# Eight fronts of a Mamba layer run first, with u, z and the dt, B, C rows kept in memory

## What is computed

```
xn    = rmsnorm(x)                       # 512 wide
u, z  = split(xn @ in_proj.T)            # 1024 wide each
u     = silu(causal_conv4(u))
dt_r, B, C = split(u @ x_proj.T)         # 32, 16, 16 wide
dt    = softplus(dt_r @ dt_proj.T + b)
h_t[n] = exp(dt*A[n]) * h_(t-1)[n] + dt*B_t[n]*u_t      # for 16 states n
y     = (sum_n h_t[n]*C_t[n] + u*D) * silu(z)
h     = x + y @ out_proj.T
h     = h + (silu(rmsnorm(h) @ w1.T) * (rmsnorm(h) @ w2.T)) @ w3.T
```

## Time and profile before

| | |
|---|---|
| median of 3 runs | 3673.43 us (3672.25 to 3678.02) |
| profiled execution | 3670.03 us, span 3668.2 us |
| PE, DVE, POOL, ACT busy | 3004.8, 2788.1, 2532.7, 2141.0 us |
| bytes moved | 497.9 MB, 136 GB/s over the span |

### The profile page before, as it was taken

How to read it: one execution, slowest core, us unless ns; L and a number is a source line. 1 busy time by engine, 2 the same in 40 slices (tenths; PEclk the granted TensorE clock), 3 DMA queues, 4 the chain that set the end, 5 groups by cost and what they waited for, 6 DMA issues and landing times. The chain is left out here.

```text
span 3668.2 us, 32780 instructions
## 1 busy us (share of the span) xinstructions
PE 3004.8 (82%) x8248; PEld 1452.7 (40%) x8248; DVE 2788.1 (76%) x3376; ACT 2141.0 (58%) x4823; POOL 2532.7 (69%) x1132
## 2 busy tenths in 40 slices
PE   6711389867986899899996899999998799999868
PEld 3200134333433444444443344444443344554444
DVE  3878889988888798879897788877898898322353
ACT  5544475567556775777558675667557756441332
POOL 0699969987988598876987677776798798300000
PEclk8855699978997999999997999999999799999979
DMA  4433445544554444554642444453555354212100
GB/s 158 122 115 127 147 142 192 171 137 153 177 169 124 133 150 141 174 166 133 203 167 93 154 135 141 157 172 135 159 175 170 123 175 143 101 42 88 39 1 23
DMA packets 225430, 497.91 MB, mean 136 GB/s; under 512 B 32348, under 2 KB 32732, under 8 KB 224988
## 3 DMA queue, kind: packets, MB, share of 16 engines
q1 hardware_dynamic: 225244, 495.82, 41.7%
HBM read 485.76 MB, written 9.96 MB: 135 GB/s over the span
## 5 line engine op out<-in xcount | busy, mean ns | idle before, releaser
L1080 POOL TENSOR_TENSOR hb<-hb,bc 128x1024 f32<-128x1024 f32 x512 | 1206.2, 2356 | 436.2 <-ACT state L1195 219.1
L1070 POOL TENSOR_TENSOR hb<-dtu,bc 128x1024 f32<-128x1024 f32 x512 | 1206.5, 2356 | 111.8 <-DVE ps L1435 107.0
L1127 ACT ACTIVATE ps<-dt,a_neg 128x512 f32<-128x512 f32 x1024 | 691.5, 690 | 687.2 <-DVE hb L1425 685.0
L1651 PE MATMUL ps<-fT,wden 128*128 128x512 f32 x2304 | 1036.2, 605 | 52.5 <-DVE dt L1413 7.5
L1425 DVE TENSOR_TENSOR_SCAN hb<-ps,hb 128x512 f32<-128x512 f32 x512 | 596.7, 1207 | 108.9 <-POOL hb L1070 96.6
L1651 PEld LDWEIGHTS ps<-fT,wden 128*128 128x128 f32 x2304 | 439.8, 194 | 600.1 <-issue 593.1
L1425 DVE TENSOR_TENSOR_SCAN hb<-ps,state,hb 128x512 f32<-128x512 f32 x512 | 627.2, 1266 | 65.5 <-POOL hb L1070 41.7
L1435 DVE TENSOR_TENSOR ps<-ps,hb 128x1024 f32<-128x1024 f32 x512 | 624.3, 1219 | 12.2 <-POOL hb L1080 11.8
L1651 PE MATMUL ps<-xnT,wmix 128*128 128x512 f32 x1024 | 456.7, 601 | 126.0 <-DMA wmix<-in_w_mix 113.4
L1741 PE MATMUL ps<-wden,hm 128*128 128x512 f32 x1024 | 456.2, 597 | 28.8 <-DVE res L1481 12.4
L1702 PE MATMUL ps<-wmix,u 128*128 128x512 f32 x512 | 241.2, 626 | 147.5 <-issue 82.0
(11 more groups left out here) (242 smaller groups left out, 3504.5 us busy)
## 6 DMA issues: line engine op xcount, KB each, us to landing
bc<-bc_dram SPq DMA_DIRECT2D x1024, 256.0 KB, 3.3
wden<-in_w SPq DMA_DIRECT2D x192, 512.0 KB, 3.9
wmix<-in_w_mix SPq DMA_DIRECT2D x128, 512.0 KB, 3.9
watt<-in_w_qof SPq DMA_DIRECT2D x26, 512.0 KB, 4.1
stage<-in_x SPq DMA_DIRECT2D x8, 1024.0 KB, 5.8
res<-in_x SPq DMA_DIRECT2D x8, 1024.0 KB, 6.6
wden<-in_w_qof SPq DMA_DIRECT2D x16, 512.0 KB, 4.2
out<-res SPq DMA_DIRECT2D x8, 1024.0 KB, 5.0
```

Of the source, the lines that this page charges most:

```text
L1070: TTn(hb[:, n % HB], dtu[:, :, :], bc[:, 0, n % BC].unsqueeze(1).broadcast_to([P, 2, CH]), ALU.mult).then_inc(s.s1_ready, 1)
L1080: TTn(hb[:, n % HB], hb[:, n % HB], bc[:, 1, n % BC].unsqueeze(1).broadcast_to([P, 2, CH]), ALU.mult).then_inc(s.s3_done, 1)
L1127: A_(dst, dt[:, p % 2, jj], ACT.Exp, scale=a_neg[:, j, n:n + 1]).then_inc(full_of(key), 1)
L1651: ins = M(dst, a, b, start=start and n == 0, stop=stop and n == len(pairs) - 1)
```

## The change

The z half of the input projection becomes a part of the front: after "proj" each front makes 8 z products, with tanh and product ("zg") as parts of the stream "f". All eight fronts come before the first output stage in that stream, with the key and value products after the first. What they make has to wait longer, so it goes to DRAM:

- a ring of two 512-wide slots (`ring`) takes the tanh of each "cvu" and "zg", the gated z, and for chunks from 2 on the dt, B, C rows. `ring_store` writes gated z to `z_dram` and the rows to `p_dram`; the next user but one of a slot waits, on ACT, until that store has landed (`ring_empty`);
- from chunk 2 on, u goes into the residual buffers `res[:, 1:3]` (`u_out`), from there to `u_dram` (`u_store`, pair by pair), and is read back into `u` (`u_load`) when the output projection has read that half of `u` for chunk c - 2;
- `z_load` reads the gated z of a pair into its place in `u` when the skip product of the pair and dt*u have been made, for the gate;
- `p_load` reads the dt rows back for chunks from 2 on; `load_b` and `load_c` read from `p_dram`;
- the third weight slot, for z, is gone: z weights go through the two slots of the fronts (`FSLOTS`);
- the residual x of chunks 1 and 2 is loaded after the last front, and "out" of chunk 0 waits for the last z product, as it shares `stage` and `xnT` with the fronts;
- the dt product waits for the skip product of the pair before, or for ACT's part of the block before.

`WORK`, `PHASE` and `LOOK` have new values, so the order of all streams is planned anew. The diff, cut to its core:

```diff
+RING = 2
@@ front
-    return got + [("proj", c)]
+    got.append(("proj", c))
+    for j in range(JB + 1):
+        got += [("z", c, j)] if j < JB else []
+        got += [("zg", c, j - 1)] if j else []
+    return got
@@ f_plan
-    got = front(0) + front(1)
+    got = []
+    for c in range(CHUNKS):
+        got += front(c)
+        if c == 0:
+            got += [("key", 0, c4) for c4 in range(KC)] + [("value", 0, b) for b in range(BATCH)]
     for c in range(CHUNKS):
...
         got += [("rms", c), ("hs", c)] + [("to", c, n) for n in range(KC)]
-        got += front(c + 2) if c + 2 < CHUNKS else []
@@ l_plan
-        for j in (2 * p, 2 * p + 1):
-            got += [("z", c, j), ("zt", c, j), ("zg", c, j)]
@@ planner's constants
-WORK = {"x": 1534.0, "w": 127.4, "s": 422.9, "y": 661.5, "f": 650.3}
+WORK = {"x": 849.2, "w": 145.7, "s": 1219.5, "y": 59.6, "f": 162.7}
-LOOK = {"m": 0.379, "l": 0.018, "x": 0.019, "w": 0.041, "s": 0.247, "y": 0.171, "f": 0.0}
+LOOK = {"m": 0.319, "l": 0.0, "x": 0.0, "w": 0.043, "s": 0.009, "y": 0.096, "f": 0.0}
@@ loads
+    for u, n in RING_AT.items():
+        if u[0] != "cvu":
+            at(DONE[u], 1, "ring_store", u)
+    for c in range(CHUNKS):
+        for p in range(PAIRS):
+            at(max(DONE[("yp", c, p)], DONE[("zg", c, 2 * p + 1)] + 4), 1, "z_load", c, p)
+            if c > 1:
+                at(DONE[("cvu", c, 2 * p + 1)], 2, "u_store", c, p)
+                at(max(DONE[("ou", c - 2, 1, p)], DONE[("cvu", c, 2 * p + 1)] + 4), 2, "u_load", c, p)
+        if c > 1:
+            at(max(DONE[("dt", c - 2, JB - 1)], DONE[("proj", c)] + 4), 2, "p_load", c)
@@ SBUF and DRAM
-        wmix = sb("wmix", [P, FSLOTS + 1, 1024])
+        wmix = sb("wmix", [P, FSLOTS, 1024])
+        ring = sb("ring", [P, RING, CH])
+        u_out = res[:, 1:3].rearrange("p r t d -> p (r t) d")
-        bc_dram = nc.dram_tensor("bc_dram", (2, 2 * NS, CH), f32, kind="Internal").ap()
+        p_dram = nc.dram_tensor("p_dram", (CHUNKS, 96, CH), f32, kind="Internal").ap()
+        u_dram = nc.dram_tensor("u_dram", (CHUNKS, PAIRS, P, 2, CH), f32, kind="Internal").ap()
+        z_dram = nc.dram_tensor("z_dram", (CHUNKS, PAIRS, P, 2, CH), f32, kind="Internal").ap()
@@ SP
+            def store_ring(unit):
...
+                sp.dma_start(dst, src).then_inc(ring_out[RING_AT[unit] % RING], 16)
@@ ACT
                 elif kind == "cvu":
                     act.wait_ge(s.conv_done, c * JB + i + 1)
-                    if i >= 2:
-                        emptied(act, ("u", c, i - 2))
-                    A_(th[:, i % 2], ps[:, USE[("u", c, i)][0]], ACT.Tanh).then_inc(s.th_ready, 1)
+                    ring_empty(act, unit)
+                    A_(ring_slot(unit), ps[:, USE[("u", c, i)][0]], ACT.Tanh).then_inc(s.th_ready, 1)
...
-                elif kind == "zt":
+                elif kind == "zg":
                     src = filled(act, ("z", c, i))
...
+                    ring_empty(act, unit)
+                    A_(ring_slot(unit), src, ACT.Tanh, scale=0.5).then_inc(s.zt_ready, 1)
                 elif kind == "out":
                     emptied(act, ("out", c, i))
                     if i == 0:
-                        filled(act, ("z", c, JB - 1))
+                        filled(act, ("z", CHUNKS - 1, JB - 1))
@@ DVE
                 elif kind == "gate":
                     summed(dve, c * STEPS + NS * i + NS - 1)
+                    dve.wait_ge(zg_in[i], 16 * (c + 1))
...
-                    V.scalar_tensor_tensor(u[:, half, i], zt, 1.0, ps[:, USE[key][0]], ALU.add, ALU.mult
+                    V.scalar_tensor_tensor(ring_slot(unit), ring_slot(unit), 1.0, ps[:, USE[key][0]], ALU.add, ALU.mult
@@ PE, dt
+                    if i % 2:
+                        pe.wait_ge(s.w_ready, c * JB + i)
+                    elif c or i:
+                        n, p = pair_of(c * PAIRS + i // 2 - 1)
+                        filled(pe, ("yp", n, p, 1))
```

More of the change, by code:

```diff
@@ L81, in l_plan, with ring_plan, ring_free @@
     got = sp_plan(0, 0) + sp_plan(0, 1)
-    for n in range(CHUNKS * PAIRS):
+    for n in range(1, CHUNKS * PAIRS):
         c, p = pair_of(n)
-        for j in (2 * p, 2 * p + 1):
-            got += [("z", c, j), ("zt", c, j), ("zg", c, j)]
-        if n + 1 < CHUNKS * PAIRS:
-            c, p = pair_of(n + 1)
-            got += sp_plan(c, 2 * p) + sp_plan(c, 2 * p + 1)
-    return got
+        got += sp_plan(c, 2 * p) + sp_plan(c, 2 * p + 1)
+    return got
+def ring_plan():
+    uses = []
+    for u in f_plan():
+        if u[0] in ("cvu", "zg") or u[0] == "proj" and u[1] > 1:
+            uses.append(u)
+    return {u: n for n, u in enumerate(uses)}, uses
+RING_AT, RING_USE = ring_plan()
+def ring_free(u):
+    n = RING_AT[u] - RING
+    if n < 0:
+        return None
+    old = RING_USE[n]
+    return old if old[0] == "cvu" else ("ring_out", old)
 def swiglu(c):
@@ L102, in y_plan @@
 def y_plan():
-    got = [("key", 0, c4) for c4 in range(KC)] + [("value", 0, b) for b in range(BATCH)]
+    got = []
     for c in range(CHUNKS):
@@ L217, in parts @@
     elif kind == "gate":
-        part(DVE, 1.5, ("zg", c, 2 * i + 1), ("sum", c, NS * i + NS - 1))
+        part(DVE, 1.5, ("z_load", c, i), ("z_kept", c, i), ("sum", c, NS * i + NS - 1))
     elif kind == "ou":
@@ L858, in f_in, with ring_slot, ring_stored, ring_empty @@
             return wmix[:, n % FSLOTS]
-        def z_in(eng, n):
-            eng.wait_ge(wz_in, 16 * (n + 1))
-            return wmix[:, FSLOTS]
+        def ring_slot(unit):
+            return ring[:, RING_AT[unit] % RING]
+        def ring_stored(eng, unit):
+            n = RING_AT[unit]
+            stored = [m for m in range(n % RING, n + 1, RING) if RING_USE[m][0] != "cvu"]
+            eng.wait_ge(ring_out[n % RING], 16 * len(stored))
+        def ring_empty(eng, unit):
+            n = RING_AT[unit] - RING
+            if n < 0:
+                return
+            old = RING_USE[n]
+            if old[0] == "cvu":
+                emptied(eng, ("u", old[1], old[2]))
+            else:
+                ring_stored(eng, old)
+        def u_there(eng, c, p):
+            if c > 1:
+                eng.wait_ge(u_in[p], 16 * (c - 1))
+            else:
+                for j in (2 * p, 2 * p + 1):
+                    emptied(eng, ("u", c, j))
+        def proj_kept(eng, c):
+            if c > 1:
+                ring_stored(eng, ("proj", c))
+            else:
+                eng.wait_ge(s.proj_stored, 16 * (c + 1))
         def y_in(eng, n):
@@ L1683, in _ @@
                         emptied(pe, ("u", c, j))
-                        ins = M(dst, wx[:, j], u[:, half, j], start=j == 0, stop=j == JB - 1)
+                        ins = M(dst, wx[:, j], u_out[:, j] if c > 1 else u[:, half, j], start=j == 0, stop=j == JB - 1)
                     ins.then_inc(full_of(key), 1)
```

177 lines of the change are left out of this document (113 added, 64 removed), and 10 rows, old and new, of the table PHASE.

## The result

The changed kernel takes 3610.1 us (median of 4 runs, 3603.7 to 3617.4), beside 3672.8 for the kernel before: a ratio of 0.983, with an interval of 0.980 to 0.985. The forecast was 3607 us. The sum is right within 3 us, and that closeness is partly luck: two of its terms were off by 27 and 18 us, in opposite directions, and the profiled execution, 3614.1 us, lies 10 above the 3604 that was forecast for it. The rest of this document is about these terms, and about a rival that was weighed by a rule that the runs overturn.

A forecast was written before the change was run, and what follows sets the result against it. No engine is full; scans, delayed 26 us by each front, then PE's tail set the end. 3670 - 21 (scans) - 45 (tail) = 3604, with the runs' median 3.4 above: 3607 us, range 3500 to 3745.

The forecast's parts named there:

- a rival that was weighed by a rule that the runs overturn: Fronts end late and delay chunk 2, from 6.2 us per z product on; near no change, 3668 us; chance 0.08.
- What chunks 0 and 1 cost: Scans of chunks 0 and 1, with seven fronts and z beside them: 822 us instead of 695, chunk 2 starting at 910.
- The prediction's lower bound: Chunks 0 and 1: fronts partly fit DVE's free 17%, each costing 14 us; scans end 100 us earlier than forecast.
- Chunks 2 to 6 then lose a front each: Later scans: 26 us less per chunk, 1995 to 1865 us; with chunk 7 and z given back, 2222 for chunks 2 to 7.
- Tail 45 us shorter: After the scans: 47 us of foreign PE work leaves chunk 7's dense stage; tail 45 us shorter, between 0 and 60.
- A front of 88 us: Fronts beside chunks 0 and 1: 61 us without z plus 27.6 for z; seven fronts end near 725 us.
- there is room until 910, 21 us a front: Between the fronts' end near 725 us, plus 35 for chunk 0's output stage, and chunk 2's start: 21 us spare a front.
- the prediction's own threshold of 109 us a front: Fronts of 88 us with 21 us of room each: late fronts cost time only from 6.2 us per z product on.
- New transfers: nothing, as long as they aren't late: DMA for z and u: 59 MB and 156 more issues on SP cost nothing if on time; uncovered u about 35 us once.
- The ring: Two-slot ring in the fronts: no bound; rival that ACT is held by its stores, 154 us, 3761 us; chance 0.31 with other order-made waits.
- The price of 3.0 us for a 256 KB store: Ring stores: 3.0 us on a line between 64 KB (2.5) and 1024 KB (5.0); slot turn somewhat over 4.4 us.
- The "much faster" rival: Scans and tail both gain: six chunks at 350 us end the scans 120 us earlier, 3487 us; chance 0.11.

The follow-up runs named there:

- The products left out: Changed kernel with the second of each four products of the last feed-forward matrix (128 dense products) left out: 3571.7 us, ratio 0.972 to the kernel before.
- run with z twice: Changed kernel with each z product of fronts 1 to 7 made twice by PE, order untouched: 3746.4 us, ratio 1.021 to the kernel before.
- run with the norm ahead: Changed kernel with norm and turning of the next front planned ahead of this front's z products: 3601.5 us, ratio 0.981 to the kernel before.
- the old values: Changed kernel with the WORK, PHASE and LOOK values of the kernel before, so another order of all queues: 3741.7 us, ratio 1.020.
- four slots: Changed kernel with a ring of four slots instead of two, planned order untouched: 3605.9 us, ratio 0.982 to the kernel before.
- one tap less: One of three DVE convolution taps left out, order untouched: changed kernel 3588.3 us (ratio 0.978), kernel before 3660.1 us (0.997).
- tiny transfers: Changed kernel with 80 extra 4 KB memory-to-memory transfers beside the u stores and the u and z loads: 3613.1 us, ratio 0.985.

## Why the prediction was right, and where its steps failed

The forecast of a small gain, with the tail as its main place, held. That the sum came within 3 us of the median is luck: the scans ended 27 us later than forecast against the kernel before, and the tail was 18 shorter. Its steps one by one:

1. **What chunks 0 and 1 cost: right in the sum, less so in its parts.** 822 against 821 us, from 26 us a front, 16 for z and 20 for other dense work. Two windows of the changed kernel, from the first dt*u to the last z tanh and from there to chunk 2, show where it was lost:

```profile
92.00:820.00 728.00, 555.86 (x1236) 245.91 (x1236) 612.10 (x675) 462.26 (x848) 523.42 (x226) 0.87 0.56 184
820.00:913.50 93.50, 74.55 (x177) 32.87 (x176) 79.78 (x79) 50.70 (x76) 92.12 (x42) 0.93 0.68 217
```

At 2.29 us for a POOL instruction, 226 of them leave 210 us of the first window, for 198 forecast for seven fronts and z. In the second POOL keeps the free pace although the dense stage of chunk 0 has begun: the 20 us put down for it weren't paid. To count a front's cost in windows in which one runs was the right way. The prediction's lower bound, 14 us from DVE's free share, would have been wrong by 100 us.

2. **"Chunks 2 to 6 then lose a front each", 130 us, and 18 for z: the mis-sized term.** They and chunk 7 lost 124 (2374 to 2250), not 148. By chunk it was 24, 6, 31, 35 and 25 us, each where 29 were forecast, and 2 in chunk 7 where 3 were forecast for its z. The one that falls out is chunk 3, which took 387 us after 393. What has changed beside it is the dense work: the feed-forward products of chunk 1 ran from 854 to 1124 us, in chunk 2, and now run from 1125 to 1361, so into chunk 3, and the means of the first batch entry begin at 1424 instead of 1175 us. So a row less its front isn't a row of the new kernel: dense work that has been put off comes in. But chunk 2 got such work too (758 PE instructions for 722, though its front is gone) and still gained 24 us, and no run moved this work alone, so that it is the reason for chunk 3 isn't shown. With this term, and a first dt*u 4 us later, the last gate comes 6 us later, not 21 earlier.

3. **"Tail 45 us shorter": too small by 18.** The mechanism is the one foretold. Nearly all of the foreign work went: the dense stage fell from 234 to 182 us, 5 below the 187 of the sum. The 187 was too high, an eighth of all products of these lines, of which 168 us lie in the stage (112 and 56 by PE's groups between 3220 and 3454 us before), so the foreign work was some 60 us and not 47. That is 7 of the 18 us. A further 7 us went between gate and dense stage and 4 behind it, which the prediction didn't count. The products left out confirm that this stretch is PE's.

4. **"A front of 88 us", and "there is room until 910, 21 us a front": failed.** A front took 103 us. From projection to the next norm it is 29 to 36 us instead of 27.6, and some 5 of them are PE's wait for z weights. That the fronts and z now share two weight slots is the likely reason, though no run gave the third slot back; the prediction gave it no price. Another 4.5 us a front are front products that took longer, 492.7 for 456.7 us in all eight; the granted clock was 0.87 over the fronts' stretch, for 0.95, 0.98 and 1.00 in the three windows beside fronts before. The rest lies in norm, turning and conv beside the scans. By the prediction's own threshold of 109 us a front this was still free. The run with z twice overturns the threshold: a front longer by 19 us (projections every 122.6 us there, every 103.6 in the changed kernel; PE's 28 us more fill the wait for z weights too, which is gone there) costs 137 / 7 = 20 us each, already in chunk 0. And the run with the norm ahead shows it from the other side, at six tenths. The step looked at the data dependence (u of chunk 2 needs the output stage of chunk 0, which needs the fronts), and not at the queues in which front and scan parts stand in one order.

5. **"New transfers: nothing, as long as they aren't late": held for the places, doubtful for the bytes.** The bytes of 80 transfers of 512 KB cost 24 us, 0.3 us each. What the change's own transfers cost wasn't measured: POOL's waits for B and C rows are 6 to 8 us in the changed kernel, for 4 before, and of the larger waits for transfers ACT's 21 us for the ring's stores are worth some 4 us by the medians, and PE's 44 us are for weights.

6. **The ring, and the rivals.** The ring hardly holds ACT: 21 us of waits for its stores, and some 4 us of time, not clear of the noise. The rival's mechanism, a part that stands in ACT's queue and holds the scans behind it, is seen in the run with z twice, but what ACT waited for was PE's product, not the store. The price of 3.0 us for a 256 KB store was too low by 1.5. The prediction had put aside the Trainium skill's page "DMA: Bandwidth & Descriptors", section "Anatomy of one DMA", which says that completion can be late above all when the target is HBM. The trace is divided: at 256 KB the store takes 4.5 us and the load 3.4, as the page has it, but at 512 KB the store of u takes 3.4 and the load 5.2. The turn of a slot is then about 6.5 us against 6.9 of PE, which just holds. The "much faster" rival (350 us a chunk) was met by one chunk of six.

What the prediction lacked is a price for the plan: with the old values the same structure is 2% slower than the kernel before. Its forecast held only because the values came with the new order, and nothing in the profile of before could show how good they were.

Open: how the 137 us of the run with z twice divide between the queues of ACT, DVE and PE (dt products and fronts share PE's too) wasn't separated. How the kernel before would do with values searched anew wasn't run. What sets the length of chunks 2 to 7 wasn't found: they take 348, 386, 365, 379, 390 and 378 us, within 4 us, in the changed kernel and in the runs with four slots, one tap less, z twice and tiny transfers, whatever happens before them.

## What to carry to other kernels

Where several streams stand in one fixed order in the engines' queues, don't count on a stream having room of its own: here fronts that became 116 us longer cost the scans 137, long before a data dependence would have made them wait, fronts 27 us shorter gave back 16, and work taken from DVE or PE gave back a quarter to a half. So price a moved stage by windows of the old trace in which it runs among the same neighbours, and don't expect every row to lose the stage's full price. Look also at the buffers that the moved parts now share: with two weight slots instead of three PE waited some 5 us for weights in each front. And try a new structure only with an order planned for it: here the values of the order were worth 131 us, twice the gain.

## What the runs showed of the hardware that was not expected

A store of 256 KB from SBUF to memory landed after 4.5 us (median of 64), while 512 KB stores of u landed after 3.4, 256 KB broadcast loads also after 3.4 and 512 KB loads of u after 5.2. The rows of the z store are 2 KB and those of u 4 KB; whether that is the reason wasn't tried. And transfers that nothing waits for are not free in a kernel whose windows show the DMA engines busy for 0.49 to 0.59 of the time: 80 of them with 512 KB cost 24 us more than 80 with 4 KB.
